# Leaving the column means to the weights, and squaring the context on ScalarE, in a three-layer graph network

## The reference

```python
u = jnp.einsum('bld,bmd->blm', h, h) / jnp.sqrt(jnp.asarray(d, h.dtype))
p = jax.nn.softmax(u, axis=-1)
delta = p * adjacency
attn = delta / (jnp.sum(delta, axis=2, keepdims=True) + 1e-10)
h_left = jnp.einsum('bld,ed->ble', h, W_left) + b_left      # also h_self, h_right
ctx = (attn above the diagonal) @ h_left + diag(attn) * h_self + (attn below the diagonal) @ h_right
mu = jnp.mean(ctx, axis=-1, keepdims=True)
var = jnp.mean(jnp.square(ctx - mu), axis=-1, keepdims=True)
o = (ctx - mu) / jnp.sqrt(var + LN_EPS) * gamma + beta
return jax.nn.relu(o)
```

## Time and profile before

| | |
|---|---|
| median of three runs | 1233.54 us |
| the profiled execution's own time | 1233.29 us |
| its span, first to last instruction | 1231.5 us |
| mean granted TensorE clock | 0.996 |
| TensorE busy | 1215.2 us, 99% |
| VectorE busy | 1089.2 us, 88% |
| ScalarE busy | 833.1 us, 68% |
| GpSimd busy | 326.8 us, 27% |

### The profile page before, as it was taken

One profiled execution on the slowest core, in us unless ns is written; L12 is line 12 of the kernel. 1 busy time (PEld: TensorE's weight loads), 2 busy tenths in 40 slices (PEclk: granted clock), 3 DMA queues, 4 the chain that ended last, 5 costly groups with the idle time before them and its releaser, 6 DMA issues.

```text
span 1231.5 us, 26747 instructions
## 1 busy us (share of the span) xinstructions
PE 1215.2 (99%) x7163; PEld 1208.6 (98%) x7163; DVE 1089.2 (88%) x3127; ACT 833.1 (68%) x2079; POOL 326.8 (27%) x439
## 2 busy tenths in 40 slices
PE   7899999999999999999999999999999999999997
PEld 6899999999999999999999999999999999999997
DVE  6799888888887799999999999999999999999986
ACT  6577767666666667776766666676666666676764
POOL 1234232222222123321212121232323232323221
PEclk9999999999999999999999999999999999999999
DMA  5444232324232234333333323322332323232321
GB/s 179 135 121 129 89 114 83 118 82 119 83 106 91 94 99 130 116 100 104 96 106 96 107 85 103 129 85 95 97 107 98 106 95 99 96 97 98 99 91 54
DMA packets 112922, 127.18 MB, mean 103 GB/s; under 512 B 11104, under 2 KB 100192, under 8 KB 112864
## 3 DMA queue, kind: packets, MB, share of 16 engines
q1 hardware_dynamic: 112864, 126.50, 32.8%
HBM read 76.91 MB, written 49.55 MB: 103 GB/s over the span
## 4 chain that ended last, share of the span: by engine, by line
PE 97%; DMA 1%; issue 1%; DVE 1%; SPq 0%; ACT 0%; POOLq 0%; POOL 0%; DVEq 0%; ACTq 0%
PE right_bank L448 25%; PE left_bank L448 24%; PE context_bank L448 24%; PE context_bank L479 17%; PE score_bank L423 6%; PE score_bank L431 1%; DMA rows<-weights 1%; DMA nodes<-squares 0%; PE edge_bank L438 0%; ACT side_parts L610 0%; DVE context L872 0%; SPq L340 0%; DVE rows L881 0%; DVE stats L844 0%; DVE turned L744 0%
## 5 line engine op out<-in xcount | busy, mean ns | idle before, releaser
L448 PE MATMUL left_bank<-weight,node_t 128*128 128x384 f32 x1728 | 338.1, 339 | 0.0
L448 PE MATMUL right_bank<-weight,node_t 128*128 128x384 f32 x1728 | 335.0, 338 | 2.2 <-DVE weight L827 2.2
L448 PE MATMUL context_bank<-weight,node_t 128*128 128x384 f32 x1728 | 332.3, 337 | 3.1 <-ACT context_bank L616 3.1
L610 ACT ACTIVATE side_parts<-right_bank 128x384 fp32r<-128x384 f32 x192 | 94.4, 492 | 317.3 <-PE context_bank L479 317.1
L448 PEld LDWEIGHTS context_bank<-weight,node_t 128*128 128x128 f32 x1728 | 303.0, 188 | 3.7 <-ACT context_bank L616 3.4
L448 PEld LDWEIGHTS left_bank<-weight,node_t 128*128 128x128 f32 x1728 | 304.3, 188 | 0.0
L448 PEld LDWEIGHTS right_bank<-weight,node_t 128*128 128x128 f32 x1728 | 299.4, 188 | 3.5 <-issue 2.6
L479 PE MATMUL context_bank<-side_parts,attn_t 128*128 128x386 f32 x1152 | 240.0, 344 | 2.2 <-issue 1.9
L479 PEld LDWEIGHTS context_bank<-side_parts,attn_t 128*128 128x128 f32 x1152 | 198.9, 189 | 4.5 <-issue 3.6
L748 DVE TENSOR_TENSOR node_t<-nodes,node_t 128x768 fp32r<-128x768 f32 x94 | 121.6, 1294 | 18.2 <-ACT node_t L558 18.2
L1034 POOL TENSOR_TENSOR edge_block<-edge,tri 128x512 f32<-128x512 f32 x96 | 131.9, 1374 | 0.0
(11 more groups left out here) (78 smaller groups left out, 1519.6 us busy)
## 6 DMA issues: line engine op xcount, KB each, us to landing
squares<-turned SPq DMA_DIRECT2D x94, 384.0 KB, 2.7
nodes<-squares SPq DMA_DIRECT2D x376, 96.0 KB, 2.2
rows<-x SPq DMA_DIRECT2D x64, 384.0 KB, 3.7
out<-rows SPq DMA_DIRECT2D x31, 384.0 KB, 2.6
adj_in<-adj SPq DMA_DIRECT2D x96, 64.0 KB, 1.9
piece<-weights SPq DMA_DIRECT2D x18, 192.0 KB, 2.5
rows<-weights SPq DMA_DIRECT2D x3, 576.0 KB, 8.5
vector_rows<-vectors SPq DMA_DIRECT2D x3, 384.0 KB, 5.3
```

What stands on the lines that cost most here:

```text
L448: mm = nc.tensor.matmul(bank[:, 0:D], node_t[:, s.parity, k, c, a], weight[:, s.phase % 2, w, c, b], start=False, stop=(c, a) == (CH - 1, ...
L610: nc.scalar.activation(side_parts[:, side, HI, 0:D], side_bank[side][k][:, 0:D], ACT.Copy).then_inc(side_hi[side], 1)
```

## The change

In the second and third phase (`level()`: all steps of them but the very last) the kernel makes the mean of `ctx` vanish instead of measuring it. From each row of a weight piece its mean over the 384 output features is taken off, and the same from the three bias rows; a context made of such projections has a mean of zero up to rounding. ScalarE does this in two instructions for a piece: one that writes a scaled copy and sums it (`accum_out`, which gives minus the mean), and one that adds this to the piece. A bias row is treated in the same way (`level_bias`, in steps g = 28 to 30). VectorE, in place of GpSimd, makes the low part of a piece. The nine pieces are spread over nine steps, g = 3 to 11, and `walk` writes twelve steps out instead of eight.

With the mean gone, `bn_stats` and the gathering fall away in these phases; `centre` is a plain product of the bank with gamma, and ScalarE then squares the bank in place with a sum (`square`), which gives the variance. `seed_self` waits for this square. VectorE's order changes as well, as shown below. TensorE's work is the same, GpSimd loses only the pieces.

```diff
-PIECES_IN = {3: 2, 4: 2, 5: 2, 6: 2, 7: 1}
+PIECES_IN = {g: 1 for g in range(3, 3 + PIECES)}
+BIAS_IN = {PAIRS - 4: RIGHT, PAIRS - 3: LEFT, PAIRS - 2: SELF}
...
-        for half in range(first, first + 4):
+        for half in range(first, first + 6):
...
@@ scalar engine
             def seed_self(s, k):
 
                 bias_row_here(s, k, SELF)
-                at_least(act, centred, s.tile(k) - 1)
+                prev = s.ahead(-1)
+                if prev.exists() and prev.level():
+                    act.wait_ge(squared, prev.tile(k) + 1 - 2 * PAIRS)
+                else:
+                    at_least(act, centred, s.tile(k) - 1)
...
                 act.wait_ge(piece_in[n % 2], 16 * (n // 2 + 1))
-                nc.scalar.activation(piece_part(phase, i, HI), piece[:, n % 2], ACT.Copy).then_inc(piece_hi, 1)
+                nc.scalar.activation(piece_part(phase, i, HI), piece[:, n % 2], ACT.Copy, scale=-1.0 / D,
+                                     accum_out=piece_mean[:, n % 2:n % 2 + 1]).then_inc(piece_averaged, 1)
+                act.wait_ge(piece_averaged, n + 1)
+                nc.scalar.activation(piece_part(phase, i, HI), piece[:, n % 2], ACT.Identity,
+                                     bias=piece_mean[:, n % 2:n % 2 + 1]).then_inc(piece_hi, 1)
...
+            def square(s, k):
+
+                act.wait_ge(centred, s.tile(k) + 1)
+                act.wait_ge(spread_done, s.n)
+                nc.scalar.activation(context_bank[k][:, 0:D], context_bank[k][:, 0:D], ACT.Square, scale=float(D) ** -0.5,
+                                     accum_out=moments[:, k, 1:2]).then_inc(squared, 1)
...
                 if nxt.exists():
                     split_nodes(nxt)
+                if prev.exists() and prev.level():
+                    square(prev, 0)
                 split_side(s, 0, RIGHT)
...
                 seed_side(s, 1, LEFT)
+                if prev.exists() and prev.level():
+                    square(prev, 1)
                 if len(pieces) > 0:
                     split_piece(*pieces[0])
+                if bias_of(s) is not None:
+                    level_bias(s.phase + 1, bias_of(s))
                 split_side(s, 1, RIGHT)
...
                     exponentials(nxt)
-                if len(pieces) > 1:
-                    split_piece(*pieces[1])
...
@@ vector engine
+            def split_piece(phase, i):
+                n = (phase - 1) * PIECES + i
+                dve.wait_ge(piece_hi, n + 1)
+                nc.vector.scalar_tensor_tensor(piece_part(phase, i, LO), piece[:, n % 2], piece_mean[:, n % 2:n % 2 + 1],
+                                               piece_part(phase, i, HI).bitcast(F32), ALU.add, ALU.subtract).then_inc(piece_lo, 1)
...
             def spreads(s):
 
-                dve.wait_ge(moments_done, s.tile(2))
+                if s.level():
+                    dve.wait_ge(squared, s.tile(2) - 2 * PAIRS)
+                else:
+                    dve.wait_ge(moments_done, s.tile(2))
...
-                dve.wait_ge(moments_done, s.tile(k) + 1)
                 at_least(dve, post_done, s.tile(k) - 1)
+                if s.level():
+                    dve.wait_ge(context_product, s.tile(k) + 1)
+                    nc.vector.tensor_tensor(context[:, k], context_bank[k][:, 0:D], vector_row(s.phase, ROW_GAMMA),
+                                            ALU.mult).then_inc(centred, 1)
+                    return
...
-                if prev.exists():
+                if prev.exists() and prev.level():
+                    denominator(prev, 1)
+                    squared_denominator(prev)
+                    centre(prev, 1)
+                elif prev.exists():
                     context_stats(prev, 1)
                     denominator(prev, 1)
...
-                if prev.exists():
+                if prev.exists() and prev.level():
+                    spreads(prev)
+                if prev.exists() and not prev.level():
                     norm(prev, 0)
                 if nxt.exists():
                     sum_scores(nxt)
...
+                if len(pieces) > 0:
+                    split_piece(*pieces[0])
+                if prev.exists() and prev.level():
+                    norm(prev, 0)
                 if prev.exists() and prev.phase > 0:
                     residual(prev, 0)
                 split_side(s, 1, RIGHT)
                 if prev.exists():
                     norm(prev, 1)
-                context_stats(s, 0)
+                if not s.level():
+                    context_stats(s, 0)
                 denominator(s, 0)
+                if s.level():
+                    centre(s, 0)
...
@@ gpsimd
-                if len(pieces) > 0:
-                    split_piece(*pieces[0])
-                if len(pieces) > 1:
-                    split_piece(*pieces[1])
```

More of the change, by code:

```diff
@@ L82, in ahead, with level @@
         return Step(self.phase, self.half + parity // 2, parity % 2)
+    def level(self):
+        return self.phase > 0 and self.ahead(1).exists()
     def exists(self):
@@ L111, in pieces_of, with bias_of @@
     return [(s.phase + 1, first + i) for i in range(PIECES_IN[s.g])]
+def bias_of(s):
+    if not isinstance(s.n, int) or s.phase + 1 == PHASES or s.g not in BIAS_IN:
+        return None
+    return BIAS_IN[s.g]
 def walk(eng, body):
@@ L117, in walk @@
         first, last = phase * PAIRS // 2, (phase + 1) * PAIRS // 2 - 1
-        for half in range(first, first + 4):
+        for half in range(first, first + 6):
             body(Step(phase, half, 0))
             body(Step(phase, half, 1))
-        with eng.Fori(first + 4, last - 1) as half:
+        with eng.Fori(first + 6, last - 1) as half:
             body(Step(phase, half, 0))
@@ L353, in body @@
                     load_residual(s)
+                if isinstance(s.n, int) and s.g == 8 and s.phase + 1 < PHASES:
+                    load_bias_rows(s.phase + 1)
                 if isinstance(s.n, int) and s.g == PAIRS - 3 and s.phase + 1 < PHASES:
-                    load_bias_rows(s.phase + 1)
                     load_norm_rows(s.phase + 1)
@@ L597, in bias_row_here @@
                 if isinstance(s.n, int) and s.g == 0 and k == 0:
-                    act.wait_ge(first_bias_in[w] if s.phase == 0 else bias_rows_in[s.phase % 2], 16)
+                    if s.phase == 0:
+                        act.wait_ge(first_bias_in[w], 16)
+                    else:
+                        act.wait_ge(bias_levelled, 3 * s.phase)
             def seed_side(s, k, side):
@@ L665, in body @@
                     return first_step(s)
-                nxt, third = s.ahead(1), s.ahead(3)
+                prev, nxt, third = s.ahead(-1), s.ahead(1), s.ahead(3)
                 pieces = pieces_of(s)
@@ L844, in context_stats, with by_stats @@
                 nc.vector.bn_stats(stats[:, k], context_bank[k][:, 0:D]).then_inc(stats_done, 1)
+            def by_stats(s, k):
+                return s.tile(k) if s.phase == 0 else 2 * PAIRS + k
             def gather_moments(s, k):
-                dve.wait_ge(stats_done, s.tile(k) + 1)
+                dve.wait_ge(stats_done, by_stats(s, k) + 1)
                 nc.vector.memset(gate[:, 2 + k:3 + k], 0.0)
@@ L860, in centre @@
                     dve.wait_ge(norm_rows_in[s.phase % 2], 16 * (s.phase // 2 + 1))
-                dve.wait_ge(moments_done, s.tile(k) + 1)
                 at_least(dve, post_done, s.tile(k) - 1)
+                if s.level():
[3 more added lines that the diff above has]
+                    return
+                dve.wait_ge(moments_done, by_stats(s, k) + 1)
                 nc.vector.scalar_tensor_tensor(context[:, k], context_bank[k][:, 0:D], moments[:, k, 0:1],
@@ L919, in body @@
                 prev, nxt, third, fourth = s.ahead(-1), s.ahead(1), s.ahead(3), s.ahead(4)
+                pieces = pieces_of(s)
                 diagonal(s)
@@ L930, in body @@
                     spreads(prev)
+                if s.phase == 2 and fourth.exists() and fourth.bounded:
+                    input_stats(fourth, 0)
+                    input_stats(fourth, 1)
                 if third.exists():
@@ L934, in body @@
                 split_edges(s)
-                if prev.exists():
+                if prev.exists() and not prev.level():
                     centre(prev, 1)
-                if fourth.exists() and fourth.bounded:
+                if s.phase < 2 and fourth.exists() and fourth.bounded:
                     input_stats(fourth, 0)
                     input_stats(fourth, 1)
-                if prev.exists():
+                if prev.exists() and prev.level():
+                    spreads(prev)
+                if prev.exists() and not prev.level():
                     norm(prev, 0)
@@ L954, in body @@
                     norm(prev, 1)
-                context_stats(s, 0)
+                if not s.level():
+                    context_stats(s, 0)
                 denominator(s, 0)
+                if s.level():
```

(7 more changed lines are left out.)

23 lines of the change are left out of this document (17 added, 6 removed).

## The result

| | before | after |
|---|---|---|
| median of six runs | 1233.14 us | 1241.76 us (1240.44 to 1242.69) |
| ratio, with 95% interval | 1 | 1.0079 (1.0068 to 1.0090) |
| span of the profiled execution | 1231.5 us | 1240.5 us |
| TensorE / VectorE / ScalarE busy | 1215.2 / 1089.2 / 833.1 us | 1221.1 / 1022.9 / 915.1 us |
| mean granted TensorE clock | 0.996 | 0.995 |

A forecast was written before the change was run, and what follows sets the result against it. TensorE was taken to bound the kernel, the change acting only through its waits. 3.1 + 6.3 - 0.7 - 0.5 = +8.2 us on 1233.3 gave 1241.5 us; own range 1238 to 1244, eight in ten 1235 to 1247.

The forecast's parts named there:

- What bounds, and what the change can do: Whole kernel: TensorE busy 1215.2 of 1231.5 us; the change acts only through TensorE's waits and can gain at most 2.3 us.
- Plain steps: Eighteen second-phase steps without a weight piece: the later shift of the scores stalls each by 0.17 us, 3.1 us.
- delay: VectorE in the second phase: the new order makes the shift of the scores come 0.48 us later (2.90 against 2.42).
- slack: Ordinary second-phase step: W1 has 2.19 - 1.88 = 0.31 us to spare before a later shift costs TensorE time.
- Piece steps: Nine second-phase steps, g = 3 to 11: VectorE's piece adds 0.53 us before the shift; each stalls 0.70, 6.3 us.
- the stretch: VectorE's instructions from L779 (place_max) to the shift of the scores (L786), second phase: 2.42 us before, 2.90 forecast.
- The four steps of 12.77: Second-phase steps near 490 us, held up by GpSimd's second piece: pieces leave GpSimd, so -4 x 0.17 = -0.7 us.
- The three steps of 13.14: Near the second phase's end, VectorE also takes third-phase input statistics: between none and all of 1.6 returns; a third, -0.5 us.
- Squares and pieces on ScalarE, third phase: ScalarE's squares and pieces or bias rows hidden in idle time; third phase loses statistics but no TensorE wait changes: 0.
- The late square: Rival, chance 0.12: ScalarE's square ends 0.4 us later, holding joined scores back 0.2 us in thirty steps; 14.2 us, 1247.5.
- The relief of VectorE: Rival, chance 0.07: fewer VectorE instructions shrink the second phase's long steps to 12.60 us, nothing new appears; 1231.0 us.

The follow-up runs named there:

- all moves made: Changed kernel with split_side between norm and residual of tile 0, centre of tile 0 behind the shift, VectorE's piece at the step's end: 1230.14 us, ratio 0.9982.

## Why the prediction was right, and where a term was off

- **What bounds, and what the change can do.** Right: only the waits of TensorE moved, and nearly all of it in the second phase.
- **Plain steps, 18 x 0.17 = 3.1 us.** The mechanism was right and the size too small: the two written-out ones cost 0.10 and 0.11, the sixteen looped ones 0.28 on the average, 4.6 us in all. Two numbers in it were off and partly made up for each other. The delay in a looped step was 0.65, not 0.48, because of the loop's 0.24 at `residual` (and 0.07 less at `place_max`). And the slack was 0.38, not 0.31: I took it from one late, written-out step and set it against looped steps. In the loop it is 0.31 in one step of the body and 0.45 in the other (2.19 less 1.88 and 1.74); the written-out steps have a shift that comes 0.07 us sooner to begin with.
- **Piece steps, 9 x 0.70 = 6.3 us.** They cost 5.6. Again the slack: the stretch is 3.36 long, 1.01 more than 2.35, less 0.38 is 0.63.
- **The four steps of 12.77, -0.7.** Right, they lost that cause when the pieces left GpSimd. That the piece was the cause was read from the waits, not tried alone. It fits that the fifth step with pieces before, which has only one, takes 12.60.
- **The three steps of 13.14, a third back, -0.5.** Measured -0.54. That was a choice between bounds, and its closeness is luck. Both parts named there were real, and they cancel: the joined scores start 0.21 us behind the start of the pair (804.03 in such a step after) in place of 0.70 (794.72 before), and from `place_max` to the shift it is 3.09 us in place of 2.61.

```profile
795.42 0.60 DVE L765 TENSOR_TENSOR score<-score_bank,cross 64x128 f32<-64x128 f32 x2
...
804.24 0.61 DVE L817 TENSOR_TENSOR score<-score_bank,cross 64x128 f32<-64x128 f32 x2 [0.31 <-PE score_bank L450]
```

  What came back, 0.18 a step, lay outside this stretch: from L0 to the next pair it is 5.60 us, where it was 5.78 in these steps before. With the order mended all of the 1.6 came back.
- **Squares and pieces on ScalarE, third phase, 0.** Right: 1.58 us idle remain behind the second square in a plain looped step, and the third phase takes 12.48 a step.
- **The rivals.** The late square did not happen: its sum ends 0.1 us ahead of `spreads`, and the joined scores start with the end of the pair. But it came nearer than forecast: `spreads` ends 0.13 us ahead of the joined scores (662.37 and 662.50), where about 0.2 had been reckoned. The relief of VectorE, which the Trainium skill's page "Perfetto Trace Analysis", section "Optimizing Scalar/DVE Operations", speaks for, did not decide as the change was ordered. With all moves made the kernel is 2.2 us faster than before, but that does not show the rule at work. Some 0.7 us of it are the four steps of 12.77, which lost GpSimd's pieces, and VectorE took these over. The other 1.6 are the three long steps, where the statistics left VectorE but `norm` of tile 0 (0.61 us) also left its place ahead of the joined scores. Whether the lighter load was needed, or order alone would do it in the kernel before, was not tried.

The spans differ by 9.0 us where 8.2 had been forecast, and the median lies 0.3 us from the forecast. That closeness is in part luck: plain steps cost 1.5 us more than forecast and piece steps 0.7 less, which partly cancel, and the first phase, the third and the drain changed by nothing together.

## What to carry to other kernels

An engine that is nearly full is not relieved where it matters by taking work off it, if the order then puts other work between a message's arrival and its answer. Find the ring that ties the engines from step to step, measure its slack, and put nothing into it that can stand outside; a cheap dummy instruction in the ring measures the slack directly, and two sizes of it give the line. Take the slack from steps of the same kind, looped or written out, as those that it is used for.

## What the runs showed of the hardware that was not expected

- One VectorE instruction, `residual`, starts later in a loop than written out: 0.88 us behind `norm`, for which it waits, in place of 0.64 or 0.65, and 0.32 us behind the shift, for which it does not wait, in place of 0.18. Behind `split_side` (0.56 long, not waited for) it starts after 0.48 in the loop too. Two other instructions that wait for the one directly ahead of them in the same loop pay nothing. Which part of `residual` it is was not settled.
- A 128x384 operation of `norm`'s kind in the second phase is followed after 0.53 us by the denominator and after 0.64 by `split_side`, neither of which depends on it; `residual` takes 0.46 ahead of `norm` and 0.59 ahead of `split_side`. What sets it was not settled.
- A square of 128x384 in PSUM took 0.46 us and the read of its sum 0.20. Adding a per-partition value to a 128x384 row in SBUF, which waits for such a sum, took 0.62 and began 0.23 us behind the start of that read.
